# A decoder layer on one core: order of the first head tiles and the last cross-attention batch in the preparation

## The reference

```python
x = _layernorm(x + _L0_attn_ref(x, ...))            # 32 heads of 16, int4-quantised projections
x = _layernorm(x + _L0_xattn_ref(x, ctx_1024, ...)) # weights from ctx_1024 alone
x = _layernorm(x + _L0_ffn_ref(x, ...))             # Hadamard rotation, 8-bit rows, ternary weights
```

```python
result, ch_bias, n = _chunk_decompose(hidden_states.reshape(bsz * tgt, H))
def proj(w_orig, w_dq_t, b):
    y = result @ w_dq_t + ch_bias @ w_orig.astype(jnp.float32).T
    return y.reshape(-1, H)[:n] + b
attn = jnp.einsum('bqhd,bkhd->bhqk', Q, K)
probs = jax.nn.softmax(attn, axis=-1)
```

```python
query = jnp.einsum('bnc,dc->bnd', teacher_features, Wq) + bq
key = jnp.einsum('bnc,dc->bnd', teacher_features, Wk) + bk
energy = jnp.einsum('bnd,bmd->bnm', query, key)
attention = jax.nn.softmax(energy, axis=-1)
x_m = jnp.einsum('bln,bmn->blm', teacher_logits, attention)
```

## Time and profile before

| what | value |
|---|---|
| median of 3 runs | 1088.88 us (1086.02 to 1090.52) |
| the profiled execution's own time | 1086.8 us |
| its span, first to last instruction | 1084.9 us |
| PE busy | 936.8 us (86%) |
| DVE busy | 875.3 us (81%) |
| ACT busy | 678.9 us (63%) |
| POOL busy | 231.3 us (21%) |
| mean granted TensorE clock | 0.959 of full speed |
| end of the preparation block | 130.2 us after the start |

### The profile page before, as it was taken

How to read it: one execution, slowest core, us unless ns; L and a number is a source line. 1 busy time by engine, 2 the same in 40 slices (tenths; PEclk the granted TensorE clock), 3 DMA queues, 4 the chain that set the end, 5 groups by cost and what they waited for, 6 DMA issues and landing times. The chain is left out here.

```text
span 1084.9 us, 13454 instructions
## 1 busy us (share of the span) xinstructions
PE 936.8 (86%) x4128; PEld 358.6 (33%) x4128; DVE 875.3 (81%) x1670; ACT 678.9 (63%) x1115; POOL 231.3 (21%) x248
## 2 busy tenths in 40 slices
PE   3567699999999999999898879897989889889966
PEld 1223233322222222222222444353444334343422
DVE  7997688899999999999897589658755776578467
ACT  3787688888888889877666234354524553275351
POOL 4203411122222331232201422140005000320001
PEclk9688899999999999999999999999999999999988
DMA  8956765566666556664442323120233004100501
GB/s 328 383 179 238 222 177 162 178 190 197 190 196 192 162 175 196 197 184 144 132 123 91 116 70 75 41 104 1 60 96 117 1 7 139 48 2 3 172 20 39
DMA packets 90684, 145.00 MB, mean 134 GB/s; under 512 B 12339, under 2 KB 52147, under 8 KB 89078
## 3 DMA queue, kind: packets, MB, share of 16 engines
q1 hardware_dynamic: 90614, 144.16, 42.3%
HBM read 84.75 MB, written 42.21 MB: 117 GB/s over the span
## 5 line engine op out<-in xcount | busy, mean ns | idle before, releaser
L402 DVE TENSOR_REDUCE neg_max<-banks 128x1 f32<-128x512 f32 x512 | 327.7, 682 | 32.8 <-PE banks L374 29.2
L1396 ACT ACTIVATE probs<-banks 128x512 f32<-128x512 f32 x512 | 277.1, 606 | 76.7 <-PE banks L1299 75.8
L1313 PE MATMUL banks<-probs,v_st 128*32 128x512 f32 x1024 | 137.9, 612 | 0.6 <-ACT probs L1396 0.6
L1850 PE MATMUL banks<-q_T,f_int_all 128*128 128x512 bf16 x512 | 122.9, 379 | 14.1 <-DVE h_ring L1871 10.1
L374 PE MATMUL banks<-attn_T,x_T 96*128 96x512 bf16 x256 | 98.6, 393 | 19.6 <-DVE neg_max L402 13.6
L1195 POOL TENSOR_TENSOR rstd<-vare,half 128x1 f32<-128x1 f32 x48 | 29.2, 608 | 401.1 <-DVE vare L1187 401.1
L1865 ACT ACTIVATE h_ring<-h_ring 128x512 f32<-128x512 f32 x64 | 40.3, 630 | 106.1 <-DVE h_ring L1860 106.1
L374 PE MATMUL banks<-k_st,q_st 96*128 96x512 bf16 x256 | 98.3, 384 | 7.8 <-DVE neg_max L402 6.4
L1299 PE MATMUL banks<-q_st,k_st 99*128 99x512 bf16 x256 | 96.0, 383 | 3.8 <-ACT probs L1396 1.8
L1299 PE MATMUL banks<-x_T,attn_T 99*128 99x512 bf16 x256 | 97.9, 382 | 0.1
L409 POOL TENSOR_TENSOR rest<-y,parts 128x512 f32<-128x512 f32 x32 | 37.6, 1174 | 211.7 <-ACT parts L382 211.6
(11 more groups left out here) (286 smaller groups left out, 1555.1 us busy)
## 6 DMA issues: line engine op xcount, KB each, us to landing
f_int_all<-in_ffn_dram SPq DMA_DIRECT2D x24, 512.0 KB, 7.6
qk_parts<-parts SPq DMA_DIRECT2D x32, 384.0 KB, 2.6
woT<-in_ffn_dram SPq DMA_DIRECT2D x24, 512.0 KB, 6.5
qk_parts<-parts SPq DMA_DIRECT2D x32, 256.0 KB, 2.9
pv_rows<-pv_z SPq DMA_DIRECT2D x32, 256.0 KB, 5.5
hz<-h_turned SPq DMA_DIRECT2D x32, 256.0 KB
x_T<-qk_parts SPq DMA_DIRECT2D x16, 384.0 KB, 3.9
attn_T<-qk_parts SPq DMA_DIRECT2D x16, 384.0 KB, 4.9
```

What stands on the lines that cost most here:

```text
L402: dve.tensor_reduce(neg_max[:, g.h, tile:tile + 1], s_bank[(16 * g.n + tile) % SB], AX.X, ALU.max, negate=True).then_inc(max_done, 1)
L1313: last = pe.matmul(pv_bank[32 * j:32 * j + 32, :], v_st[g.v][:, kt].rearrange("p h d -> p (h d)")[:, (HD + 1) * head:(HD + 1) * head + 2 * ...
L1396: act.activation(probs[ktp][:, j, i, :], st_bank[(16 * g.n + 2 * w + i) % STB], ACT.Exp).then_inc(exp_done, 2)
L1850: last = pe.matmul(bank, f_int[w][:, k * FF + ch.start:k * FF + ch.stop], q1_T[:, k, :], start=k == 0, stop=k == KD - 1)
```

## The change

Nothing is added or taken away. In three engines' lists work changes places:

- PE's `pe_energy` is cut into `pe_xqk` and `pe_energies`. For batch 3 the product of `tile0`, c = 1 (with its wait for `bias_step` 12) now stands between the two, in front of the energies.
- DVE scales that product (`dve_y(dve, tile0, 1, ...)`) before it takes the maxima of batch 3's energies, not after.
- ACT makes the high and the middle part of `tile0`, c = 1, before it divides batch 2 and copies its turned parts out; the spread of o's scales (`act_spread(act, 3)`) stands between the two parts.

```diff
-            def pe_energy(pe, B):
+            def pe_xqk(pe, B):
...
+
+            def pe_energies(pe, B):
                 need(pe, "xqk_sb", 2 * B + 2)
                 for n in range(KD):
                     did(pe.matmul(E_BANK[n], xqk[:, 0, n * P:(n + 1) * P], xqk[:, 1, :], start=True, stop=True), "e_mm")
+
+            def pe_energy(pe, B):
+                pe_xqk(pe, B)
+                pe_energies(pe, B)
...
                     act_row(act, 2)
+                    act_high(act, tile0, 1)
+                    act_spread(act, 3)
+                    act_middle(act, tile0, 1)
                     act_divide(act, 2)
-                    act_spread(act, 3)
-                    act_high(act, tile0, 1)
                     act_turn(act, 2)
-                    act_middle(act, tile0, 1)
                     act_exps(act, 3)
...
                     pe_rows(pe, 2)
-                    pe_energy(pe, 3)
+                    pe_xqk(pe, 3)
                     pe.wait_ge(bias_step, 12)
                     pe_qk(pe, tile0, 1, TURN_BANK[1])
+                    pe_energies(pe, 3)
                     pe_rows(pe, 3)
                     pe.wait_ge(y_ready, 2)
                     pe_turn(pe, 2)
...
                     weight_scale(3)
+                    dve_y(dve, tile0, 1, TURN_BANK[1])
                     dve_energy_max(dve, 3)
-                    dve_y(dve, tile0, 1, TURN_BANK[1])
                     weight_round(3)
```

## The result

The changed kernel ran at 1092.36 us, median of 20 runs (1086.48 to 1097.73), beside 1087.69 us for before, median of 20 (1083.06 to 1090.88): ratio 1.0036, 95% interval 1.0020 to 1.0052. Two more sets of the same kernel, 12 runs each, gave means 2.1 us (0.2 to 4.0) and 4.5 us (2.1 to 7.0) above their runs of before; by means, the first set is +3.9 us (2.3 to 5.5). Weighted together the three sets give +3.4 us (2.3 to 4.5), 0.3%. The forecast was 1089.7, +0.8, with a range of 1086.0 to 1093.5 and 0.93 on "within 0.5%": the sign is right, the three sets together stay within 0.5%, the time lies inside the range, and the size is four times too small.

The account below looks back on a forecast made before the run. No single engine bounds it; PE's own queue replaces the first score's data wait, and DVE and POOL end the block. Block +1.0 us, less what the clock gives back, is +0.8: 1088.88 + 0.8 = 1089.7 us, range 1086.0 to 1093.5.

Parts of the forecast that it names:

- within 0.5%: Whole kernel: time stays within 5.4 us of before, about what measurement can tell from no change; chance 0.93.
- What bounds the kernel: Preparation block: the first score's 3.10 us data wait is all that can be saved; DVE and POOL end it 0.17 us apart.
- The parts before the scores: Preparation: data 4.03 us sooner, batch 2's turn 2.20 us late, first score 1.04 and first maximum 0.62 us sooner.
- the product at half clock: PE's k half product: starts at 98.62, runs at half clock, and DVE scales at 100.95 instead of 103.80.
- full-clock bound: PE's k half product at full clock: ACT's chain only 1.1 us late, block within 0.1 of before, total +0.1.
- The scores: Score tiles: PE waits for ACT before batch 3's parts 0 and 2, DVE is held, block ends +1.0 us.
- The next stage: Stage after the block: starts 1.0 us later, clock may give back 0.5; bounds +0.5 and +1.0, taken +0.8.
- the length of PE's wait: PE's clock: idle times of 1.55 and 1.75 us kept full clock, 2.02 brought half; new 1.46 us, so no fall.
- (a): Scores: batch 3's parts don't hold DVE, so nothing is given back; -0.6 us, 1088.3, chance 0.20.
- (c): PE's new wait before batch 2's turn: the clock falls once more; +2.5 us, 1091.4, chance 0.12.
- (d): PE's new wait before batch 2's turn: clock falls and stays half through tile1's products; +0.8 and 9.5, 1099, chance 0.03.
- (b): Before the scores: the whole 3.10 us wait goes, PE arriving as before; -3 us, 1085.9, chance 0.03.

Follow-up runs that it names:

- before_again: The kernel before, unchanged, measured again with a second profile: -0.3 us (-1.7 to +1.2) against before.
- warm_before: The kernel before with dummy matmuls filling PE's waits in the preparation: +0.6 us (-1.6 to +2.7) against before.
- late_before: The kernel before with batch 3's turned parts two score tiles later and ACT's tile1 parts ahead of their copies: -0.2 us (-2.4 to +2.0) against before.
- late_after: The kernel after with batch 3's turned parts two score tiles later and ACT's tile1 parts ahead of their copies: +3.8 us (2.1 to 5.4) against before.
- late_divide_first: The kernel after with batch 2's division ahead of the k half's parts, plus the two edits of late_after: +0.7 us (-1.1 to +2.5) against before.
- act_alone: The kernel before with only ACT's reordering, PE and DVE keeping their old order: +4.5 us (2.8 to 6.1) against before.
- pe_dve_alone: The kernel after with ACT's old order restored, so only PE's and DVE's reordering: +2.4 us (0.8 to 4.0) against before.
- after_third: The kernel after, unchanged, a third set of runs: +4.5 us (2.1 to 7.0) against before.
- after_again: The kernel after, unchanged, a second set of runs: +2.1 us (0.2 to 4.0) against before.

## Why the prediction was right or wrong

**What bounds the kernel.** Right: the wait of the first score for its data went, PE's queue took its place, and the block ended with two ends close together, POOL at 130.50 and DVE at 129.82.

**The parts before the scores.** The order of events was as forecast, each 0.8 to 0.9 us sooner: scaling at 1.55 us from the split step for the forecast 2.44, the middle part at 4.28 for 5.18. The step that failed is the product at half clock: I carried the half stretch of the one profile to the same place, and it began 0.92 us after the product's start (98.21 for 97.29), as the windows row of after shows (stretch, length, PE busy, granted clock, DMA share, GB/s):

```profile
98.21:101.62 3.41, 3.41 (x6) 0.50 0.09 21
```

The turn of batch 2 stands 7.47 behind the split step for 8.29, so v's bias product is 1.34 us late and not 2.20. The forecast's full-clock bound fails too. It gave ACT's chain 1.1 us late and the block level with before, +0.1; the product came close to that case, and measured against the same profile of before the block ends 0.4 us later in two profiles of after and 1.6 in the first, which ran 6.83 us of its scores at half clock (118.69 to 125.52). And eight records of energies take 3.60 to 3.70 us at full clock, not the 3.44 of the sum.

**The comparison with before.** This is the term that was mis-sized, and the other way. I took 104.60 for the turn in before as if the schedule gave it. Half clock in the energies had made it 1.3 us late, and in executions without that (before_again, warm_before, late_before: v's bias product at 7.33, 7.32, 7.32) before is that much quicker, while after stays at 9.8 to 10.0 with its energies at full or at half clock. So the right price at this point is 1.3 to 2.7 us, not one number, and at the block's end +0.4 to +3.2 over the pairs of unfilled profiles; I took +1.0. The same goes for the gain: the first maximum, forecast 0.62 us sooner, is 1.4 to 1.5 sooner than in the one profile of before and 0.4 later than in the other. The mean of after's three is 32.8, of before's two 31.2: +1.6.

**The scores.** Right in mechanism and place: 0.90 us before part 0 (forecast about 1), a wait before part 2 released by ACT, DVE's ninth maximum held. late_after confirms by its own failure that these copies are what DVE waits for.

**The next stage.** I took the clock to give 0.2 us back. No run shows that: from the next block's start to v's third product it is 6.60 and 6.74 us in the profiles of before and 6.30, 6.87 and 6.90 in those of after.

**The rule of the clock.** On this the Trainium skill, "TensorE: Matmul & The Clock Gate", Part 1, was weighed and only bounded: it says that the monitor runs free of the kernel's start. The traces agree, with the half stretch at 98.44 in one profile of before and none from 86 to 114 in the other. The prediction's other guide, the length of PE's wait, fails in them: 2.64 us of waiting (2.65 in one) stand before the product in after's three profiles, in late_after and in late_divide_first, and in the first four the clock fell to half within 1 us of the product's start, in the last it stayed up. I used the page's sentence for the spread of after's time alone; it bears as much on before's, and there it changed the result.

**The rivals.** (a), nothing is given back: didn't come. (c) and (d), the clock falling at PE's new wait: didn't come; the wait was 0.59 us, not 1.46, and the bias product took 3.62 us at full clock in after. (b), the whole wait goes: no. The bin with the chance 0.93, "within 0.5%", is the right one by the means; the bounds of the first and the last set reach just beyond it.

**What stays open.** The block accounts for about 1.6 us (0.4 to 3.2), and the three sets gave +3.9, +2.1 and +4.5. act_alone and pe_dve_alone, with blocks 4.5 and 2.8 us behind the mean of before's two, cost 4.5 and 2.4, nothing more than their blocks. So 1 to 2 us of after's cost aren't accounted for, and the stretch behind the block shows nothing in the profiles (957.1 and 957.5 us). After's runs spend some 6 us more at half clock than before's by their mean clocks (0.9523 to 0.9534 for 0.9551 to 0.9565); whether the shifted block makes the later stretches long more often, or the sets were unlucky, these runs can't say. Few profiles stand for many runs here: one of each kernel, three of after and two of before.

## What to carry to other kernels

A step that has to wait for another engine holds up everything behind it in its own engine's list: here ACT's division of 2.56 us had stood in a free slot, and behind the parts it held PE's turn by 1.3 to 2.7 us; most of what the earlier data gained PE's queue took anyway. With the division put back in front the cost was gone as far as the runs can tell (+0.4, -2.0 to +2.8). Keep ready work that others wait for in front of waiting work when an engine works strictly through its list. And before a few microseconds are argued from one profile, take a second one of the same kernel: here the half-clock stretch lay elsewhere, and the chain through TensorE was 1.3 us shorter in one than in the other.

## What the runs showed of the hardware

- The same program's energies took 5.40 us in one execution and 3.70 in another; the difference is the granted clock (0.50 for 3.42 us in the one, 1.00 throughout in the other).
- Filling TensorE's waits with dummy products kept the clock at 1.00 from 92 to 126 us (mean over the runs 0.959 for 0.9565), and no gain could be measured: +0.6 us (-1.6 to +2.7).
- The same wait of 2.64 us (2.65 in after_third) before the same product was followed by half clock in four profiles (after, after_again, after_third, late_after) and by full clock in a fifth (late_divide_first).
- The same instructions behind the first attention took 499.48 us in one execution and 503.41 in another, at 0.96 and 0.95 mean clock; PE's busy time there was 428.17 and 432.22 us.
